# Windowed attention, strip by strip: score matmuls regrouped around the transposed maxima, and key copies moved in the DMA order

## What is computed

```
x = x + conv_branch(LN_c(x))         # windowed attention, then an MLP with a 5x5 depthwise conv
t = tokens(x); t = t + ffn(LN(t))    # quantized feed-forward, 96 -> 384 -> 96

conv_branch: windows of 16x16 with step 14 (19 x 19 windows per image, overlapping)
  y = LN(tok) ; q, k = y@wq, y@wk (4 heads x 16) ; v = y@wv (4 heads x 24)
  attn = softmax(q k^T / 4) ; tok = (attn v) @ wproj + tok
  overlapping windows are averaged
```

## Time and profile before

| | |
|---|---|
| median of 3 runs | 9297.89 us |
| runs | 9271.66, 9297.89, 9303.39 us |
| the profiled execution's own time | 9312.9 us |
| its span, first to last instruction | 9311.1 us |
| mean granted TensorE clock | 0.950 of full |
| PE busy | 8116.5 us, 87% |
| PEld busy | 4895.6 us, 53% |
| DVE busy | 5242.7 us, 56% |
| ACT busy | 4650.3 us, 50% |
| POOL busy | 2129.6 us, 23% |

### The profile page before, as it was taken

The page is one execution under the profiler, slowest core; times in us unless marked ns, Lnnn a source line. Parts: engine busy times, 40 slices in busy tenths (PEclk is TensorE's granted clock), DMA queues, the critical chain, the costliest instruction groups (busy, mean ns, idle before and its releaser), DMA issues. The chain is left out here.

```text
span 9311.1 us, 207757 instructions
## 1 busy us (share of the span) xinstructions
PE 8116.5 (87%) x76932; PEld 4895.6 (53%) x76932; DVE 5242.7 (56%) x9929; ACT 4650.3 (50%) x8702; POOL 2129.6 (23%) x1712
## 2 busy tenths in 40 slices
PE   6775899999998999999958988899889989888998
PEld 3333444444444444444436666666666666666665
DVE  5565777777777777777734444444444444444444
ACT  2221555555555555555525555555555555555554
POOL 0000333333333333333311211112111212111121
PEclk8887999999999999999969999999999999999999
DMA  4343333333333333333351111111111111111110
GB/s 118 111 121 105 85 87 83 93 90 82 90 92 81 90 91 85 87 92 84 86 47 40 36 40 40 42 33 43 39 43 33 43 39 37 40 41 42 33 43 23
DMA packets 480809, 612.70 MB, mean 66 GB/s; under 512 B 173262, under 2 KB 415696, under 8 KB 455316
## 3 DMA queue, kind: packets, MB, share of 16 engines
q1 hardware_dynamic: 480260, 605.46, 26.6%
HBM read 395.81 MB, written 166.64 MB: 60 GB/s over the span
## 5 line engine op out<-in xcount | busy, mean ns | idle before, releaser
L810 DVE TENSOR_REDUCE NM<-P 128x2 f32<-128x512 f32 x2888 | 1910.2, 688 | 738.6 <-PE P L642 730.0
L757 ACT ACTIVATE PROB<-P 128x512 f32<-128x512 f32 x2888 | 1491.1, 603 | 1217.0 <-PE P L657 1217.0
L1204 PE MATMUL P<-FC,XN 97*126 97x192 f32 x5408 | 1114.7, 346 | 15.7 <-ACT Y L1366 14.8
L1204 PEld LDWEIGHTS P<-FC,XN 97*126 97x126 f32 x5408 | 959.3, 199 | 168.6 <-issue 79.0
L642 PE MATMUL P<-KB,QB 32*128 32x256 bf16 x5776 | 864.4, 280 | 197.8 <-DVE QF L804 105.9
L657 PE MATMUL P<-QF,KS 32*128 32x256 f32 x11552 | 953.9, 412 | 0.0
L642 PEld LDWEIGHTS P<-KB,QB 32*128 32x128 bf16 x5776 | 248.2, 94 | 1079.6 <-DVE QF L804 533.5
L493 POOL TENSOR_TENSOR Y<-XHS,RNS 96x512 f32<-96x512 f32 x304 | 593.1, 1982 | 934.7 <-DMA RNS<-rnorm 934.6
L1350 ACT ACTIVATE SQ<-Z 96x512 f32<-96x512 f32 x260 | 163.8, 630 | 1286.0 <-DVE Z L1500 1286.0
L665 PE MATMUL P<-PROB,V 128*32 128x256 f32 x11552 | 796.2, 394 | 1.5 <-ACT PROB L757 1.5
L1366 ACT ACTIVATE Y<-P 126x384 f32<-126x384 f32 x1352 | 709.7, 570 | 117.4 <-PE P L1204 110.2
(11 more groups left out here) (141 smaller groups left out, 12344.3 us busy)
## 6 DMA issues: line engine op xcount, KB each, us to landing
RBC<-sums SPq DMA_DIRECT2D x456, 160.0 KB, 3.1
X<-x2map SPq DMA_DIRECT2D x52, 1344.0 KB, 8.4
XHS<-xhat SPq DMA_DIRECT2D x76, 768.0 KB, 6.2
RNS<-rnorm SPq DMA_DIRECT2D x38, 1536.0 KB, 9.5
x2map<-XHS SPq DMA_DIRECT2D x76, 768.0 KB
T<-in_x SPq DMA_DIRECT2D x52, 960.0 KB
out<-T SPq DMA_DIRECT2D x52, 960.0 KB, 4.9
X<-in_x SPq DMA_DIRECT2D x32, 1536.0 KB, 13.2
```

The lines of the kernel that those rows point to most:

```text
L757: A.activation(PROB[:, par, u, :], P[:, B_ST[u], :], ACT.Exp, scale=DQ ** -0.5).then_inc(act_exp, 1)
L810: V_.tensor_reduce(NM[:, :, 32 * u + DQ], P[:, B_S[u], :].rearrange("p (a m) -> p a m", a=2), axis=AX.X, op=ALU.max).then_inc(dve_max, 1)
L1204: m = M.matmul(P[0:KW, 5 + (r + 2) % 3, i * MLP:(i + 1) * MLP], xnf[:, RI * WX * w:RI * WX * w + KW], FC1[:, :], start=True, stop=True)
```

## The change

Three edits, all in `attention_stage`.

1. The transposed maxima go to bank 0 (the bank of S^T of head 0) and no longer to bank 5. PE's `maxima` therefore waits also for the first exponential of window j-1 (`act_exp` at 4j - 3). The scores of heads 0 and 1 of window j+1 are issued together, directly behind the transposes and ahead of the chunk, with one signal; DVE's `row_max` waits for two signals per window and no longer three.
2. On DVE, `residual` stands ahead of `queries16` in the windows that have both (j = 1, 3, 5, 7, 16, 18).
3. On SP, three chunks of keys move. `spread` gets two places into which a caller can put work: `gathered` (behind the four RS loads) and `summed` (behind the DMA to `sums`, ahead of the wait for its landing). Chunk 3's keys go into `summed` of the group of the strip before (they stood behind the loads of SH and RN), chunk 5's into `gathered` of group 0 (they stood behind the whole spread), and chunk 1's of the next strip into `summed` of group 2 (they stood behind the whole spread).

```diff
-        B_ST, B_S, B_MT, B_OV, B_CK = (0, 1, 2, 3), (4, 5, 4, 5), 5, 6, 7
+        B_ST, B_S, B_MT, B_OV, B_CK = (0, 1, 2, 3), (4, 5, 4, 5), 0, 6, 7
...
-            def spread(s, n, q, first):
+            def spread(s, n, q, first, gathered=lambda: None, summed=lambda: None):
...
                       .then_inc(sums_in, 16)
+                gathered()
                 if not first:
                     hold(sp, sp_passed, pool_grp, n(s, 4, q - 1))
                 hold(sp, sp_passed, dve_rsh, n(s, 4, q + 1))
                 sp.dma_start(sums[sl, 0:HEADS * PT * nw].rearrange("(p e) -> p e", p=128), RS[:, sl, 0:8 * nw]).then_inc(recip_out, 16)
+                summed()
                 hold(sp, sp_passed, recip_out, n(s, 64, 16 * q + 16))
...
                 if prev:
-                    spread(s - 1, n, 3, False)
+                    spread(s - 1, n, 3, False, summed=lambda: keys(s, n, 3))
...
-                keys(s, n, 3)
+                if not prev:
+                    keys(s, n, 3)
                 keys(s, n, 4)
-                spread(s, n, 0, not prev)
-                keys(s, n, 5)
+                spread(s, n, 0, not prev, gathered=lambda: keys(s, n, 5))
...
-                spread(s, n, 2, False)
                 if follow:
-                    keys(s + 1, n, 1)
+                    spread(s, n, 2, False, summed=lambda: keys(s + 1, n, 1))
+                else:
+                    spread(s, n, 2, False)
...
                     pe.wait_ge(dve_max, n(s, 4 * NPOS, 4 * j + 4))
+                    if prev or j > 0:
+                        pe.wait_ge(act_exp, n(s, 4 * NPOS, 4 * j - 3))
                     maxima()
                     if more:
                         pe.wait_ge(dve_kb, n(s, NCK, NCK * ((j + 1) // NPOS) + first_new(nj) + 1))
-                        scores(nj, 0)
+                        scores(nj, 0, 1)
...
                     pe.wait_ge(dve_qf, n(s, NPOS, j + 1))
-                    if more:
-                        scores(nj, 1)
                     if prev or j > 0:
                         pe.wait_ge(act_exp, n(s, 4 * NPOS, 4 * j))
                     scores_t(j)
...
             pe.wait_ge(dve_kb, 1)
-            scores(0, 0)
-            scores(0, 1)
+            scores(0, 0, 1)
...
                 for u in range(4):
-                    if u < 3:
-                        dve.wait_ge(pe_s, n(s, 3 * NPOS, 3 * j + u + 1))
+                    if u % 2 == 0:
+                        dve.wait_ge(pe_s, n(s, 2 * NPOS, 2 * j + u // 2 + 1))
...
+                    for c, at in OUT_STEP.items():
+                        if at == j and (c < 4 or prev):
+                            residual(s - (c > 3), n, c)
                     for c, at in QK_STEP.items():
                         if at == j - 1 and (c > 1 or follow):
                             queries16(s + (c < 2), n, c)
-                    for c, at in OUT_STEP.items():
-                        if at == j and (c < 4 or prev):
-                            residual(s - (c > 3), n, c)
```

## The result

| | before | after |
|---|---|---|
| median | 9296.19 us (4 runs) | 9175.40 us (4 runs) |
| lowest to highest | 9271.66 to 9303.39 | 9146.56 to 9185.78 |
| ratio, 95% interval | 1 | 0.9872 [0.9858, 0.9887] |
| span of the profiled execution | 9311.1 | 9184.0 |
| attention, first to last QF | 3744.7 | 3618.7 |

The change makes the kernel 1.28% faster, about 119 us. The sign and the range of the prediction hold; of the 236 us that were forecast only half came. The spans differ by 127.1 us and the stretch from first to last QF by 126.0, so nearly all of it lies in the attention.

What follows compares the result with a forecast made beforehand. It took attention to be bound by a ring passing between PE and DVE, neither full, plus waits for keys and residual. The sum 96 + 33 + 80 + 45 - 18 = 236 us gave 9062 us, range 8975 to 9195.

Steps and rivals of the forecast that it cites:

- The sign: Whole kernel: faster by more than the 28 us that a measurement can tell from no change, chance 0.89.
- the likeliest mechanism: Attention: the forecast case, in which all gains and costs add up to 236 us, chance 0.52.
- A: Chunk windows: scores of heads 0 and 1 ahead of the chunk save 0.20 us in 13 windows per strip, 96 us.
- B: DVE: residual ahead of the cast frees PE's bank 7 earlier; half of a 66.3 us wait goes, 33 us.
- The new wait for the first exponential: PE's transposes wait for ACT's first exponential; with 1.1 us of cover it costs nothing.
- C: SP: chunk 3's keys ahead of RN's load remove 80 of DVE's 89.8 us key wait; the clock adds 45 us.
- The clock term of 45 us: Attention: part of the time at 1.2 GHz follows window 4's wait and goes with it, 45 us (0 to 112).
- D: Cost of the moves: RB loads and POOL's groups come later and POOL lies over DVE's copies, -18 us (0 to -73).
- The part for blocked copies: DVE copies that POOL's shifted instructions lie over lose 0.5 us per strip, -18 us.
- the key wait moves elsewhere on SP's queue: Rival: window 11's shares or window 5's projection wait instead and the clock falls there; 111 us gained, 9187, chance 0.12.
- Only the waits go: Rival: S^T fills the time, so the earlier scores gain 0; 140 us gained, 9158 us, chance 0.15.
- POOL blocking DVE's copies: Rival: six copies per strip each last 1.98 us longer, slower at 9484 us; threshold 1.14 us per copy; chance 0.06.

Runs made afterwards that it cites:

- x9: x8 with edit 1 undone (maxima in bank 5, scores of head 1 behind the chunk): 9090.30 us, ratio 0.9782.
- x1: Edit 1 alone on the kernel before: 9318.14 us, ratio 1.0041.
- x10: x8 with edit 2 undone (the cast ahead of the residual again): 9052.02 us, ratio 0.9746.
- x2: Edit 2 alone on the kernel before: 9306.27 us, ratio 1.0021.
- x11: Kernel before with only chunk 3's keys moved, behind the RB loads and ahead of SH and RN: 9200.00 us, ratio 0.9900.
- x5: Changed kernel with chunk 3's keys issued behind the RB loads of group 3, not ahead of them: 9140.52 us, ratio 0.9834.
- x3: Edit 3 alone on the kernel before: 9215.81 us, ratio 0.9921.
- x6: Changed kernel with the next strip's chunk 1 keys back behind the whole spread of group 2: 9168.71 us, ratio 0.9882.
- x7: Changed kernel with POOL making Y of chunk 0 alone ahead of group 1: 9095.65 us, ratio 0.9787.
- x4: Changed kernel with POOL making Y of chunks 0 and 1 ahead of group 1: 9128.39 us, ratio 0.9822.
- x8: Changed kernel with x5, x6 and x7 together: 9045.62 us, ratio 0.9728.

## Why the prediction was right, and where it was off

The sign and the likeliest mechanism held, and the time lies in the range. The size was off by a factor of two: 119 us where the sum gave 236. By its steps:

**A, edit 1.** The mechanism and the 0.20 us were right in the window: 0.98 us from S^T to the scores of heads 2 and 3, 4.54 us per window, 0.17 in window 14 and, with B, 0.38 in window 3. The new wait for the first exponential cost nothing: the trace puts none of PE's idle time before the transposes down to ACT. The term as a whole, 96 us, was too large: with the waits removed it is worth 50 us (x9), and on the kernel before it is worth less than nothing (x1). I had counted three windows (6, 11 or 12, and 15) as giving back their own 0.20 us and no more. Windows 6 and 11 gave back 0.36 and 0.20 us more than that, window 9 another 0.15, and in the changed kernel window 15 far more.

**B, edit 2.** PE's wait for the residual went, more wholly than forecast (66.3 us to 0 in the matmul row). It bought little time: not clear of noise, 6 to 17 us, in x10, none in x2, against 33 forecast. The step that failed is counting half of a wait as time; the next window that waits for something else gave it back (window 4 for the keys in x2, window 6 for the row sums in x10).

**C, edit 3.** Right: the wait fell by 86.5 of 89.8 us (80 forecast), and the cause was their place behind RN's load (x11: 93 us by moving only those keys past it and SH's). Issued behind it, chunk 3's copies landed 7.9 us after their issue on average; ahead of it, in the changed kernel, 2.0 us after. The clock term of 45 us was right where it was measured: window 5 of x11 is 1.22 us shorter, with a mean granted clock of 1.00. In the changed kernel it was lost again. The clock over the stage is 0.97 as before, for the low stretches moved: window 5 went from a mean of 0.81 to 0.95, window 15 from 0.99 to 0.86.

**D, the price of the moves.** This is the term that was mis-sized. I gave it 18 us. I had named the cover, 1.6 us of slack before the projection of window 5, and had said that each us past it costs 37; but I had taken it from a strip whose group 3 has fewer pieces than most, and put the step at no cost. In the changed kernel the projection was a mean 1.00 us late: x5 gives 35 us back. The part for blocked copies came out near its size by luck. L801's mean rose by 66 ns, 20 us over 303 copies, but the moves alone (x3) lowered it to 558 ns, and in x6, where it is 704 ns, the kernel is no slower. No run shows that these 20 us are time.

**What the sum did not have** is window 15. I wrote that it "waits for POOL's Y" and counted it as giving back its own 0.20 us. It takes 1.95 us more than before and 2.85 more than without the wait (x7: 79 us, of which window 11 cost some). Two things make it up. The wait stands at a point that another chain sets, so it gives back what was gained since that chain started. Counted from the issue of the DMA to `sums` to QF of window 15, that is 0.30 us in odd strips and 0.44 in even ones, and in the even ones windows 11 to 15 take 24.02 us in sum where they took 23.93. And in the odd strips the chain itself is 1.85 us later by its two transfers; there the same windows take 27.17 us where they took 23.84, 1.2 GHz for part of window 15 included. The prediction had neither the later transfers nor the clock there. That the wait is the loss is shown (x4, x7); why the transfers land later is argued in the last section, and stays open.

Of the rivals, "the key wait moves elsewhere on SP's queue" (9187) came closest in time, and window 5 shows half of its mechanism (the projection waits for what is now later). "Only the waits go" has the wrong reason, for edit 1 did its work. POOL blocking DVE's copies stayed far below its threshold of 1.14 us per copy.

**What stays open.** The x1 run was 38 us slower, while its strip sum is only 0.22 us above that of the profiled kernel before, 8 us over 37 strips. That profiled execution took 9312.9 us, 28 us above the median of the runs of before that were timed beside x1, which accounts for most of the rest. The granted clock goes with it: 0.940 to 0.946 in the seven runs of x1, 0.950 to 0.954 in the 18 of before. That edit 1 alone brings nothing is shown; how much of the 38 us is the key copies, the late transfers or the clock is not.

## What to carry to other kernels

When several engines meet at points whose time another chain sets (a load behind a large transfer, a helper engine's result), time taken out between two such points can come back at the next one, in part or whole. So tabulate the period of the loop by position, mark the positions that wait for something that is not on the loop, and credit an edit only with what lies beyond the last of them; then move that producer first. An edit that is worth nothing alone can be worth something behind such a move (edit 1: slower by 38 us alone, 50 us of gain in x8), so try edits together before they are dropped. And split the table by parity where the loop is unrolled by two: here a mean of 1.95 us was 3.72 in odd strips and 0.18 in even ones.

## What the runs showed of the hardware that I had not expected

*The wait in window 15 cost more than its own length.* In strip 21 PE idled 2.42 us, and S^T then took 2.09 us where it takes 1.15 at full clock; the window was 9.80 us against 4.57 without the wait. Over the odd strips the chunk started 2.38 us later than without the wait and the window was 4.33 us longer, at a mean granted clock of 0.77; over the even ones it was 1.05 and 1.37 us, at 0.96. The clock fell in that window in 17 of the 21 strips in which PE had idled 1.43 to 3.23 us for Y. In the other four (1.72 to 2.75 us) it did not, nor in the 15 with 0.41 to 1.26 us, so the length of the wait alone does not decide it here. Such waits in an engine that is otherwise busy were priced too low.

*An early helper instruction blocks another engine's copy.* With Y ahead of group 1, DVE's cast of window 11 took on average 1.32 us (x4) where it takes 0.42, and DVE's small product RSC<-RSC,SH there 1.12 us where it takes 0.20. The forecast had only casts and key copies on its list. The changed kernel has the same in window 1: the product takes 0.82 us there and 0.19 in the kernel before and in x6, and x6 is no faster. The Trainium skill (SBUF — State Buffer, Who interferes with whom) has a VectorE instruction with two SBUF inputs contend with a GpSimd instruction that reads SBUF; the trace agrees, with those 1.12 us.

*Transfers land later beside a packet of an instruction queue.* The DMA to `sums` before group 1 landed after 2.3 to 2.6 us in all 18 odd strips of the changed kernel, and after 1.5 to 2.7 in the even ones. The DMA view of the odd strip 21, over 3016.2 to 3018.8, has one packet of an instruction queue:

```profile
q14 instruction: 1, 0.01, 1.1%
...
sums<-RSC SPq DMA_DIRECT2D x1, 20.0 KB, 2.3
```

and that of the even strip 20, over 2918.5 to 2920.3, has none:

```profile
sums<-RSC SPq DMA_DIRECT2D x1, 20.0 KB, 1.5
```

All 152 such transfers of the changed kernel follow it, by the trace. The 87 without such a packet between issue and landing took 1.42 to 1.55 us, the 65 with one 1.65 to 3.04. (Only six have one in the kernel before, and these took 1.44 to 1.49, so it does not delay every transfer.) The RB loads of group 1 go the same way: 5.20 to 6.26 us in the odd strips, each with one such packet, and 4.51 to 5.06 in the even ones, which have none; in the kernel before it is the even strips that have the packet, with a mean of 5.22 us against 4.70. The loop body holds two strips, so a fetch of code can fall on the same place in each odd strip. Where it falls goes with edit 1: the kernels without it (before, x2, x3, x9, x11) have 2 to 14 of 152 transfers to `sums` beside such a packet, those with it 47 to 70. No run moves the fetches and nothing else, so it is argued from this, not tested, that they delay the transfers.
